# Scores ahead of the second output tile, and a reordered transfer queue, in a two-layer graph-attention kernel

## The reference

```python
def _L0_gnn_ref(seq, Wq, bq, Wk, bk, Wv, bv, Wf, bf, graph_mask):     # 6 heads of 128
    q = _heads(seq @ Wq + bq); k = _heads(seq @ Wk + bk); v = _heads(seq @ Wv + bv)
    scores = einsum('bhqd,bhkd->bhqk', q, k) / np.sqrt(HEAD_SIZE)
    probs = softmax(scores + where(graph_mask, 0.0, NEG), axis=-1)
    return einsum('bhqk,bhkd->bhqd', probs, v) ... @ Wf + bf

def _L1_gnn_ref(feat_in, adj, W, b, w_src, w_dst, H_w, H_b):          # 12 heads of 64
    h = einsum('bnd,ade->bane', feat_in, W)
    th = tanh(h)
    attn = einsum(th, w_src) + swapaxes(einsum(th, w_dst))
    attn = softmax(where(mask, -999.0, leaky(attn)), axis=-1)
    feat_out = elu(einsum('banm,bame->bane', attn, h) + b)
    gate = sigmoid(feat_in @ H_w.T + H_b)
    return gate * feat_out + (1.0 - gate) * feat_in

h = maximum(layernorm(x), 0.0);  x = x + L0(h, ...)
h = maximum(layernorm(x), 0.0);  x = x + L1(h, adj, ...)
return x
```

## Time and profile before

| | |
|---|---|
| median of three runs | 2491.99 us |
| the profiled execution's own time | 2491.45 us |
| its span, first to last instruction | 2489.6 us |
| PE busy | 2405.5 us (97%) |
| PE weight loads busy | 1714.1 us (69%) |
| DVE busy | 2176.0 us (87%) |
| ACT busy | 1091.1 us (44%) |
| POOL busy | 852.4 us (34%) |
| DMA queue, share of 16 engines | 69.9% |
| mean granted TensorE clock | 0.994 |

### The profile page before, as it was taken

The page is one execution under the profiler, slowest core; times in us unless marked ns, Lnnn a source line. Parts: engine busy times, 40 slices in busy tenths (PEclk is TensorE's granted clock), DMA queues, the critical chain, the costliest instruction groups (busy, mean ns, idle before and its releaser), DMA issues.

```text
span 2489.6 us, 58759 instructions
## 1 busy us (share of the span) xinstructions
PE 2405.5 (97%) x22408; PEld 1714.1 (69%) x22439; DVE 2176.0 (87%) x3236; ACT 1091.1 (44%) x1416; POOL 852.4 (34%) x589
## 2 busy tenths in 40 slices
PE   7898999999999999999999999999999999999997
PEld 6665676667776667776667776667776667776665
DVE  7867888988988988988988988988988988988968
ACT  6434334444444444444444444444444444444434
POOL 0223233343233343233343233343333343333331
PEclk9999999999999999999999999999999999999999
DMA  7376777776677776677776677776677776677762
GB/s 261 94 179 173 204 190 197 218 212 181 200 192 199 219 212 181 200 189 201 219 212 180 198 190 200 220 211 182 197 190 203 219 211 182 194 193 203 217 157 52
DMA packets 755673, 481.24 MB, mean 193 GB/s; under 512 B 611760, under 2 KB 636336, under 8 KB 755632
## 3 DMA queue, kind: packets, MB, share of 16 engines
q1 hardware_dynamic: 755632, 480.65, 69.9%
HBM read 277.59 MB, written 34.60 MB: 125 GB/s over the span
## 4 chain that ended last, share of the span: by engine, by line
DVE 38%; issue 24%; ACT 10%; SPq 9%; POOL 9%; DMA 6%; PE 5%; DVEq 1%; POOLq 0%; ACTq 0%
POOL arena L2644 4%; SPq L663 4%; DVE arena L1710 3%; SPq L669 3%; DVE arena L1545 3%; PE pair_prj L902 3%; DMA arena<-arena 3%; DVE bn_out L1421 3%; DVE arena L1534 2%; DVE arena L1542 2%; DVE arena L1531 2%; ACT arena L2246 2%; ACT arena L2248 2%; DVE max L1853 2%; POOL rstd L2618 2%
## 5 line engine op out<-in xcount | busy, mean ns | idle before, releaser
L902 PE MATMUL pair_prj<-w_hi,arena 128*128 128x256 f16 (+1 forms) x3432 | 810.7, 326 | 25.3 <-DVE p_place L1599 20.4
L902 PE MATMUL pair_prj<-w_lo,arena 128*128 128x256 f16 (+1 forms) x1716 | 559.6, 326 | 0.0
L902 PEld LDWEIGHTS pair_prj<-w_hi,arena 128*128 128x128 f16 x3432 | 337.0, 98 | 255.3 <-issue 32.7
L928 PE MATMUL pair_prj<-arena,w_hi 128*128 128x256 f16 x2376 | 394.2, 273 | 3.3 <-DVE arena L1465 2.3
L2649 POOL TENSOR_TENSOR arena<-arena 128x768 f32<-128x768 f32 x60 | 108.8, 1813 | 777.3 <-DVE arena L1710 555.3
L928 PE MATMUL pair_att<-arena,w_hi 128*128 128x256 f16 x2160 | 360.0, 273 | 0.0
L928 PE MATMUL pair_prj<-arena,w_lo 128*128 128x256 f16 x1188 | 324.5, 273 | 0.0
L928 PE MATMUL pair_att<-arena,w_lo 128*128 128x256 f16 x1080 | 294.4, 273 | 0.0
L1226 PE MATMUL pair_prj<-w_hi,arena 128*128 128x384 f16 x870 | 255.0, 326 | 2.8 <-DMA w_lo<-forms 1.6
L928 PEld LDWEIGHTS pair_prj<-arena,w_hi 128*128 128x128 f16 x2376 | 228.6, 98 | 30.2 <-DVE arena L1465 2.6
L902 PEld LDWEIGHTS pair_prj<-w_lo,arena 128*128 128x128 f16 x1716 | 168.6, 98 | 108.8 <-issue 1.4
(11 more groups left out here) (275 smaller groups left out, 4985.0 us busy)
## 6 DMA issues: line engine op xcount, KB each, us to landing
w_hi<-forms SPq DMA_DIRECT2D x353, 288.0 KB, 3.9
w_lo<-forms SPq DMA_DIRECT2D x353, 288.0 KB, 4.7
arena<-in_x SPq DMA_DIRECT2D x63, 768.0 KB, 4.8
out<-arena SPq DMA_DIRECT2D x64, 384.0 KB, 2.3
arena<-arena SPq DMA_DIRECT2D x31, 768.0 KB, 3.7
arena<-arena SPq DMA_TRANSPOSE x372, 3.3
forms<-w_lo SPq DMA_DIRECT2D x14, 288.0 KB, 3.2
forms<-w_hi SPq DMA_DIRECT2D x10, 288.0 KB, 3.5
```

The source lines that it names most:

```text
L902: mm = nc.tensor.matmul(pair[:, lo:hi], lhs(a, k), weight(m, k, b)[:, lo:hi], start=(k == 0 and n == 0), stop=(k == KT - 1 and n == 2))
L928: mm = nc.tensor.matmul(pair[:, c * 256:(c + 1) * 256], weight(m, k, a)[:, o:o + P], (ht0_hi, ht0_lo)[b][:, k, :], start=(k == 0 and n == ...
```

## The change

Three orders are changed; no instruction is added, removed or resized. On DVE, in steps 2 to 30, `scaled_scores` and `shift0` now stand ahead of `output_elu(1)` and `output_gated(1)`. On SP, in the loop, the two high transposes of the next state move ahead of the second store, the two low ones ahead of the copy to `keep`, and the load of `x1` between the high and the low transposes of the probabilities. In step 2, the low parts of the gate terms are computed later on DVE (T3 and T2 behind `output_first(1)`, T1 and T4 behind `p0_low`), and their stores, the form loads, the stores of the gate's quarters and the resident gate units move back on SP.

```diff
@@ SP, one() @@
+                def load_x1():
+                    after_alone(sp, eye_made, full_made[1], 2 * j + 2)
+                    after_alone(sp, eye_made, x1_moved, DMA * (2 * j + 2))
+                    sp.dma_start(x1, x_g[i]).then_inc(x1_moved, DMA)
+
                 if last:
                     store(p, 0)
+                if mid and seven_gate(j):
+                    after_held(sp, transposes_held, v_psum, 2 * i + 2)
+                    transpose_rows(0, 0, ht0_hi, i + 1)
                 if last:
                     store(p, 1)
+                if mid and seven_gate(j):
+                    transpose_rows(0, 1, ht0_lo, i + 1)
                 if now and mid:
                     after_alone(sp, eye_made, out_stored, 2 * DMA * j)
                     sp.dma_start(keep, x1).then_inc(x1_moved, DMA)
-                    if seven_gate(j):
-                        after_held(sp, transposes_held, v_psum, 2 * i + 2)
-                        transpose_rows(0, 0, ht0_hi, i + 1)
-                        transpose_rows(0, 1, ht0_lo, i + 1)
-                    after_alone(sp, eye_made, full_made[1], 2 * j + 2)
-                    after_alone(sp, eye_made, x1_moved, DMA * (2 * j + 2))
-                    sp.dma_start(x1, x_g[i]).then_inc(x1_moved, DMA)
-                if third:
-                    store_gate_lows((T1, T4))
-                    first_forms()
+                    if not seven_gate(j):
+                        load_x1()
                 if now and not first:
                     ...
                     transpose_blocks(pt0[0], e0[0], pt0_landed)
+                    if mid and seven_gate(j):
+                        load_x1()
                     after_held(sp, transposes_held, p0_lo_made, i)
                     transpose_blocks(pt0[1], e0[1], pt0_landed)
                 ...
                 elif third:
-                    store_gate_quarters()
-                    gate_residents()
+                    store_gate_lows((T1, T4))
+                    first_forms()
                 if seven(i):
                     late_forms()
+                if third:
+                    store_gate_quarters()
                 ...
                 if mid:
                     first_probabilities(j, j + 1)
+                if third:
+                    gate_residents()
@@ DVE, one() @@
                 if third:
                     gate_terms()
-                    low_gate_term(T3)
-                    low_gate_term(T2)
                 ...
                 if third or (last and mid and seven_gate(j)):
                     output_first(1, p)
+                if third:
+                    low_gate_term(T3)
+                    low_gate_term(T2)
                 ...
+                if early_values:
+                    scaled_scores()
+                    shift0()
                 if last:
                     output_elu(1, p)
                     output_gated(1, p)
-                if now:
-                    if not early_values:
-                        low_values(0)
+                if early_values:
+                    low_values(1)
+                    normal0()
+                    p0_low()
+                elif now:
+                    low_values(0)
                     ...
+                if third:
+                    low_gate_term(T1)
+                    low_gate_term(T4)
```

More of the change, by code:

```diff
@@ L2051, in one @@
                     shift0()
[L2052 to L2056, removed]
                     normal0()
-                    if second or not nxt:
-                        low_values(1)
+                    low_values(1)
                     p0_low()
+                if third:
+                    low_gate_term(T1)
+                    low_gate_term(T4)
                 if second:
```

## The result

The changed kernel takes 2529.27 us (median of four runs, 2526.99 to 2529.73) against 2492.52 for the kernel before on the same chip: ratio 1.0144, 95% interval 1.0126 to 1.0161, 37 us slower. The prediction was 2488 with a range to 2513. It was wrong.

The account below looks back on a forecast made before the run. The prediction took a ring of waits through SP's queue, 74.77 us per loop step, to bound the kernel, with PE's waits only its remainder. From 2491.45, +3 for the loop and -6.5 for step 2 gave 2488, range 2460 to 2513.

Parts of the forecast that it names:

- What bounds the kernel: PE's loop waits at `context` and `project_h(1)`, about 0.5 us each per step, are only what the ring leaves over.
- the ring: Chain of waits from one `context` to the next: 59.21 us to the copy, 15.74 back; mean step 74.77.
- the tile's stall: DVE's second-tile output before the change: its last instruction stands for POOL's L2683, 2.29 us for 0.96, losing 1.33.
- The first part of the ring: From `context` to SP's copy to `keep`: 59.21 us before, 64.0 after, the copy being 4.8 later.
- two instructions of the tile stretched: In DVE's second-tile output, two of four instructions wait for POOL's L2683, about 2.6 us lost, bounds 0 and 3.1.
- The second part, "Sum: 4.39 + 4.75 + 1.65 + 0.15 = 10.9": Copy to `context`: copy to load 4.39 us, load landing 4.75, last two transposes 0.9 and 0.75, then 0.15 to `context`.
- keeps its distance from it: All else on PE, ACT and POOL behind `context` stays as far behind it; PE waits about 1.5 us there.
- SP's high transposes as free: SP issues the state's two high transposes while it would wait for the second store, so they cost nothing.
- Slow issue rival (2504): SP's low transposes behind the store issue slowly, 0.6 us per step: +20 - 6.5, 2504; chance 0.13.
- Lost lock rival (2531): POOL's L2677 comes ahead of DVE's L1631, which loses 1.8 us; ring 1.65 longer: +46 - 6.5, 2531; chance 0.15.
- Step 2: PE waits 6.0 + 4.3 + 1.6 = 11.9 us in step 2; half comes back, 6.5, bounds 0 and 12.
- Sum: Whole kernel: 2491.45 us, +3 for 28 loop steps at about +0.1 each, -6.5 for step 2, giving 2488.

Follow-up runs that it names:

- mask_first: Kernel before, with VectorE's mask moved ahead of the second tile's output in the loop; 2493.9 us, ratio 1.0007.
- dve_only: Kernel before, with VectorE's new loop order alone, SyncE's order as before; 2652.9 us, ratio 1.0638.
- pool_waits_for_tile: Kernel before, with one wait added: in the loop POOL starts its two subtractions only when the second tile's output is done; 2457.9 us, ratio 0.9859.
- after_small_copy: Changed kernel, with the loop's copy to `keep` moving 64 of 768 columns of each tile; 2485.7 us, ratio 0.9974 to the kernel before.
- sp_only: Kernel before, with SyncE's new loop order alone, VectorE's order and step 2's splits as before; 2530.0 us, ratio 1.0141.
- after_load_last: Changed kernel, load behind all four probability transposes, POOL's `target_terms` ahead of both bias additions; 2475.9 us, ratio 0.9932 to the kernel before.
- changed_busy_pe: Changed kernel, with 8 throwaway matmuls issued on PE before its wait for the probability transposes in the loop; 2509.0 us, ratio 1.0068.
- prep_only: Kernel before, with step 2's part of the change alone, the loop as before; 2491.6 us, ratio 0.9989.

## Why the prediction was wrong

- **What bounds the kernel.** Right. As the ring has it, a wait of PE that is taken away at one place comes back at the other (mask_first), a late copy costs at least as much as it is late (dve_only), and the tile's stall comes off one for one (pool_waits_for_tile).
- **The first part of the ring.** Right: 64.0 forecast, 63.85 measured, with two instructions of the tile stretched, as worked out, and the mask free.
- **The second part, "Sum: 4.39 + 4.75 + 1.65 + 0.15 = 10.9".** This is the step that failed: two of its terms were too small. In the mean of the loop 4.90 + 5.21 + 1.59 + 0.13 = 11.8 are measured (4.95, 4.94, 1.59 and 0.13 in the step shown). The 4.39 kept the 3.19 us of the pair that stood behind the copy before, the state's high transposes, for the probability transposes that stand there now; these take 3.87. The second one was 1.67 in the earlier trace rows's group of four already (5.89 for four), and I used the 1.30 of another tile. The small copy gives 2.7 for the same pair, so the large one is the cause. This term is 0.5 of the miss. The rest is the load's landing, 5.21 for 4.75. The load now stands between the two pairs of probability transposes; where it does so too, in after_small_copy and sp_only, it lands 5.1 to 5.2 behind its issue as well, and 4.7 to 4.8 where it stands ahead of all four (before) or behind them (after_load_last). What delays it there no run takes apart. Together 0.89 a step, 24 us.
- **PE's clock.** Left out. I wrote that PE would wait about 1.5 at `context` and that all else "keeps its distance from it". It waits 1.8 to 2.6, and behind 7 of these waits in the loop PE runs at half its clock, 1.4 us each; there are two more behind the loop. In the loop they are 10 us; with PE kept busy (changed_busy_pe) the kernel is 20 us faster. So the "distance" is not kept where a wait of this length stands before it.
- **SP's high transposes as free.** Right in the changed kernel, where the late tile makes SP wait for the store; wrong as a statement on SP's order, which alone costs 1.3 a step.
- **Slow issue rival (2504).** It had the kind of cost right, and the place wrong: the low transposes behind the store take 2.60, as usual; the slow ones stand behind the copy.
- **Lost lock rival (2531).** Its number was hit by other mechanisms, by luck; L1639 kept its 0.96.
- **Step 2.** Forecast -6.5, measured about -3 (prep_only, -2.7). The 4.3 of wait at `context` went, but PE waits 6.7 instead of 6.0 for `low_values(1)` and 3.3 instead of 1.6 for the forms. That half of the 11.9 would come back was a guess.
- **Sum.** In the two traces the loop's 27 steps are 34.7 longer: +4.6 was in the forecast (74.94 against 74.77 a step, written as +3), -4 is the first part, 0.15 shorter than forecast, +24 the second part (0.89), +10 the seven half clocks. Step 2 gives 2.9 back, and the steps behind the loop, with two half clocks, take 3.7, for which the forecast had nothing: 35.5, the difference of the spans.

## What to carry to other kernels

When a loop is a ring through a transfer queue, the waits of the busiest engine are only its slack: find the chain that returns to itself, and price a change by what it adds to that chain. Look in it for instructions that are longer than their like; here one wait on the other engine was worth 35 us, twice as much as the best of the reorderings alone (after_load_last, 17). And before a wait of the matmul engine is allowed to grow, ask whether the engine comes out of it at full clock.

## What the runs showed of the hardware

- A transpose by DMA takes SP 1.24 to 1.3 us to issue. Directly behind the 768 KB copy in the same queue the two of the probabilities take 1.9 each (3.87 with the gap), the two of the state 1.84 and 1.29; behind a copy of a twelfth of that size the two of the probabilities take 2.7 together.
- A VectorE instruction with two SBUF operands waits out a running GpSimd `tensor_tensor`: 2.28 for 0.96 in the tile, once a step before and twice in the changed kernel, 1.99 for 0.96 in the scores' subtraction in pool_waits_for_tile; never where POOL's was 16 columns wide. Making POOL's `memset` small changed nothing that can be told from noise.
- Starting the GpSimd pair only when VectorE's four are done takes 3.24 instead of 3.96 for POOL, and costs VectorE 1.0 in one later instruction, where before it lost 1.33 and 1.44: serial is faster than beside each other, for both.
- In the loop the granted clock fell to 0.50 for about 3 us behind waits of PE of 2.07 to 2.58 us in the changed kernel and 1.82 to 2.08 in sp_only, and not behind every wait of that length (one of 2.49 kept 1.00); never behind those of 0.4 to 0.8 in the kernel before, nor behind those of up to 1.45 in the loops of after_small_copy and mask_first; in dve_only, with 4.7 to 5.3, in every step.
